# Folding the query weights behind the first and the third quarter of y's matmuls, and the first folded block copied out ahead of the spreading of post_ln

## What is computed

```python
h = tok(x)                         # rms_norm(2560) @ w1.T -> silu(gate) * value (512) @ w2.T -> rms_norm (1024)
h = h + attn(layernorm(h))         # 32 heads, low-rank queries (256) and keys/values (64), rotary halves, causal
h = h + ffn(layernorm(h))          # 1024 x 1024 base + 8 experts of rank 16, weighed by a router

# in attn:
q = rmsnorm(x @ wq_a.T, q_a_ln_w) @ wq_b.T            # per head 64 without and 64 with rotation
ckv, k_pe = split(x @ wkv_a.T)
kv = rmsnorm(ckv, kv_a_ln_w) @ wkv_b.T                # per head k_nope 64, v 128
scores = q_full @ k_full.T * scale ; out = softmax(scores) @ v ; return out @ wo.T
```

## Time and profile before

| | |
|---|---|
| median of 3 executions | 2593.61 us (2593.51 to 2594.55) |
| the profiled execution | 2587.67 us, span 2586.0 us, granted TensorE clock 0.974 |
| TensorE matmul busy | 2431.7 us, 94% of the span, 15004 matmuls |
| VectorE, ScalarE, GpSimd busy | 1635.5, 1187.8, 1000.5 us |
| DMA | 313.61 MB, 121 GB/s over the span |
| `tok_down` | about 640 to 965 us of the span |

### The profile page before, as it was taken

The page is one execution under the profiler, slowest core; times in us unless marked ns, Lnnn a source line. Parts: engine busy times, 40 slices in busy tenths (PEclk is TensorE's granted clock), DMA queues, the critical chain, the costliest instruction groups (busy, mean ns, idle before and its releaser), DMA issues. The chain is left out here.

```text
span 2586.0 us, 45893 instructions
## 1 busy us (share of the span) xinstructions
PE 2431.7 (94%) x15004; PEld 2111.5 (82%) x15004; DVE 1635.5 (63%) x3318; ACT 1187.8 (46%) x3624; POOL 1000.5 (39%) x852
## 2 busy tenths in 40 slices
PE   8999999986899988999999999799999997999998
PEld 6888878865566658999999999688888885899998
DVE  8875587894366657888888898511111113777775
ACT  5664444441345548999999999511111111111110
POOL 5764676772023226667666767100000001011110
PEclk9999999998899999999999999899999998999999
DMA  7654587676466541111111111533333333212211
GB/s 249 201 173 142 184 257 244 209 229 226 136 197 201 194 149 67 46 44 47 40 47 43 47 45 39 198 113 98 97 97 97 97 97 102 69 66 73 75 65 49
DMA packets 202314, 313.61 MB, mean 121 GB/s; under 512 B 20784, under 2 KB 157488, under 8 KB 202032
## 3 DMA queue, kind: packets, MB, share of 16 engines
q1 hardware_dynamic: 194256, 282.54, 34.2%
q0 software_dynamic: 7184, 25.69, 2.5%
q10 hardware_dynamic: 720, 3.67, 0.4%
HBM read 230.05 MB, written 81.79 MB: 121 GB/s over the span
## 5 line engine op out<-in xcount | busy, mean ns | idle before, releaser
L1871 POOL TENSOR_TENSOR ffn_res<-shared_h,ffn_bias 128x1024 f32<-128x1024 f32 x24 | 60.3, 2516 | 852.4 <-DMA ffn_bias<-base_b 555.9
L1512 ACT ACTIVATE attn_prob<-attn_prob,attn_bias 94x94 f32<-94x94 f32 x1024 | 366.9, 361 | 43.4 <-DVE attn_bias L1589 42.0
L740 PE MATMUL up_ps<-up_t_lo,up_s_hi 128*128 128x502 f32 (+1 forms) x840 | 333.5, 397 | 23.2 <-DVE up_t_lo L655 23.1
L741 PE MATMUL up_ps<-up_t_hi,up_s_lo 128*128 128x502 f32 (+1 forms) x840 | 329.8, 393 | 0.0
L742 PE MATMUL up_ps<-up_t_hi,up_s_hi 128*128 128x502 f32 (+1 forms) x840 | 329.0, 392 | 0.0
L1721 DVE TENSOR_TENSOR out_x_lo<-out_raw,out_x_hi 128x512 fp32r<-128x512 f32 x96 | 66.5, 692 | 399.3 <-ACT out_x_hi L1706 399.3
L506 POOL TENSOR_TENSOR up_both<-up_raw 128x502 f32<-128x502 f32 (+1 forms) x150 | 240.3, 1606 | 118.3 <-DVE up_t_lo L655 84.9
L1706 ACT ACTIVATE out_x_hi<-out_raw 128x512 fp32r<-128x512 f32 x96 | 60.6, 632 | 434.7 <-PE out_ps_h L243 284.5
L1628 POOL TENSOR_TENSOR attn_prob<-attn_prob,attn_share 94x752 f32<-94x752 f32 x128 | 184.6, 1442 | 179.5 <-DVE attn_share L1597 179.5
L243 PE MATMUL out_ps_h<-out_w_hi,out_x_lo 128*128 128x512 f32 x768 | 238.1, 391 | 11.2 <-DVE out_w_lo L228 11.2
L243 PE MATMUL out_ps_h<-out_w_lo,out_x_hi 128*128 128x512 f32 x768 | 237.3, 390 | 0.0
(11 more groups left out here) (227 smaller groups left out, 5760.5 us busy)
## 6 DMA issues: line engine op xcount, KB each, us to landing
up_raw<-x_f SPq DMA_DIRECT2D x240, 251.0 KB, 3.4
up_w_raw<-w SPq DMA_DIRECT2D x120, 256.0 KB, 4.1
up_raw<-x_f SPq DMA_DIRECT2D x120, 250.0 KB, 3.7
out_raw<-o_t SPq DMA_DIRECT2D x96, 256.0 KB, 4.3
o_t<-attn_o_t SPq DMA_DIRECT2D x128, 188.0 KB, 1.9
shared_ring<-wo SPq DMA_DIRECT2D x32, 512.0 KB, 6.6
y<-down_y POOLq DMA_DIRECT2D x24, 512.0 KB, 3.4
out_y<-y SPq DMA_DIRECT2D x24, 512.0 KB, 5.7
```

Source lines behind the costliest of these rows:

```text
L740: nc.tensor.matmul(o, sh, tl, start=(kk == 0), stop=False)
L741: nc.tensor.matmul(o, sl, th, start=False, stop=False)
L1512: last = nc.scalar.activation(prob[u % NPR][0:SEQ, h, part], prob[u % NPR][0:SEQ, h, part], ACT.Exp, bias=bias[u % 2][0:SEQ, n:n + 1], sca ...
```

## The change

Three edits, all in `tok_down`. On ScalarE `spread()` of the first body moves behind `wq_out`. On TensorE `fold_q(f, 0)` moves from ahead of y to between n = 0 and n = 1, and `fold_q(f, 1)` from between n = 1 and n = 2 to between n = 2 and n = 3. For the late fold and for steps without y, both still stand behind y's place. No instruction is added or taken away. The name of the change also speaks of paired weighing in attention; the diff holds no line of `attention`.

```diff
@@ ScalarE, body(k, m)
-                if isinstance(k, int) and k == 0 and m == CENTRE_AT:
-                    spread()
                 f = fold(k, m)
                 if f is not None:
                     p, b, turn = f
...
                     last.then_inc(f_out, 1)
+                if isinstance(k, int) and k == 0 and m == CENTRE_AT:
+                    spread()
                 s = stage(k, m, D_Y, U, TILES)
@@ TensorE, body(k, m)
                 late = f is not None and first(f[0], 1)
-                if f is not None and not late:
-                    fold_q(f, 0)
                 s = stage(k, m, D_Y, U, TILES)
...
                     for n in range(4):
-                        if n == 2 and f is not None and not late:
-                            fold_q(f, 1)
+                        if n % 2 == 1 and f is not None and not late:
+                            fold_q(f, n // 2)
                         if first(t, 1):
                             ws.wait(pe, n)
                         last = three_pass(nc, outs, g_hi[u][:, n, :], g_lo[u][:, n, :],
...
                     last.then_inc(y_made, 1)
-                if late:
+                if late or (s is None and f is not None):
                     fold_q(f, 0)
-                if late or (s is None and f is not None):
                     fold_q(f, 1)
```

## The result

The changed kernel takes **2584.09 us** (median of 20 executions, 2578.82 to 2587.95), the kernel before 2591.32 in the same comparisons (20, 2584.97 to 2596.76): ratio 0.9970, 95% interval 0.9963 to 0.9978. That is 7.2 us, 0.28%, where 7.7 was forecast.

What follows compares the result with a forecast made beforehand. TensorE was taken to pace `tok_down`, with only its 3.4 us of gaps per 67 us iteration winnable. 6.95 (B steps) + 1.8 (start) - 1.05 (A steps) = 7.7 us off the median 2593.61: 2585.9 us, range 2581.5 to 2591.5.

Steps and rivals of the forecast that it cites:

- A step: Fold step whose step ahead has no fold (m = 2, 5): loss of 0.15 us each, times 7, -1.05 us.
- B step: Fold step directly following a fold (m = 3, 0): 1.39 us won each, in five of eight, 6.95 us.
- The way back: Two B steps at m = 0 where VectorE's loop returns: its "issue" gap stays, gain taken as nothing, 2.8 us left for range.
- The start: First body, step m = 2: `wq_out` no longer behind `spread`, next fold's work earlier, 1.8 us won (0.8 to 2.6).
- rival 3: Nothing won: the gain is lost to other phases of DMAs and fetches in attention; 2593.6 us, 4%.
- Rival 4: Slower: `wq_out` too late for `fold_v(0)` with one quarter as cover; 2606.9 us at 2.2 us lateness, 4%.
- Rival 2: The wait moves on: VectorE's gap is longer or also at loop entry and exit; 2588.7 to 2591.6 us, 21%.
- Rival 1: More won: VectorE's gap shrinks with TensorE's earlier y, start reaches its upper bound; 10.5 to 11.3 us, 2583.1 us, 11%.
- L1190's wait: Sign: the fold's first matmuls wait for ScalarE's `wv_out`, falling from 11.8 us to about 1.5.
- the first `fold_v(0)`: Sign at the stage's start: it stands at about 663.5 in place of 669.50.
- transposes to `fold_v(0)`: Sign on TensorE: this stretch takes 7.8 us in B, 7.7 in A.
- L1198's wait: Sign: the fold's last matmuls wait 3.1 us growing to about 6, all in two places after VectorE's "issue" gaps.

Runs made afterwards that it cites:

- before_look: The kernel before, unchanged, profiled once more for a second look at its B steps: 2589.22 us, a single execution.
- spread_only: The kernel before with only `spread()` moved behind the first `wq_out`, folds in their old places: 2590.72 us, ratio 0.9993 to the kernel before.
- after_again: The changed kernel once more, nothing altered, in a second comparison: 2580.44 us, ratio 0.9951 to the kernel before.
- folds_only: The changed kernel with `spread()` back ahead of the first `wq_out`, so only the folds moved: 2578.64 us, ratio 0.9939 to the kernel before.
- folds_again: The same kernel as folds_only, run once more on one chip with after_again: 2583.35 us, ratio 0.9967 to the kernel before.
- q1_half: The changed kernel with `fold_q(1)` back between n = 1 and n = 2: 2581.04 us, ratio 0.9956 to the kernel before.
- flat_before: The kernel before with VectorE's steps of `tok_down` written out in place of a loop: 2587.11 us, ratio 0.9978 to the kernel before.
- flat_after: The changed kernel with VectorE's steps of `tok_down` written out in full: 2571.97 us, ratio 0.9909 to the kernel before.
- q1_last: The changed kernel with `fold_q(1)` behind all of y, right ahead of `fold_v(0)`: 2576.13 us, ratio 0.9937 to the kernel before.

## Why the prediction was right

Step times over the profiles of all kernels with the one order of folds or the other, in us:

| | before, before_look, spread_only | after, after_again, folds_only, folds_again, q1_half | by the sum |
|---|---|---|---|
| A step | 12.02 | 12.02 | +0.15 |
| B step, the five of seven not on a way back | 13.66 to 15.33, mean 14.22 | 12.26 to 12.42, mean 12.32 | -1.39 |
| B and next, on a way back | 22.33 to 24.95, mean 23.55 | 24.42 to 26.65, mean 25.36 | 0 |
| VectorE's gap there | 5.01 to 6.36 | 5.58 to 6.77 | the same |

*B steps.* The mechanism and its size were right: 13.67 to 12.27 where nothing else happened, 1.40 against 1.39. What the sum didn't have is that the wait of 1.5 us was in some steps followed by a stretch at 1.2 GHz, 1.5 us more: 5 of the 15 B steps of the first column. None of the 25 of the second had one. So the mean gain of a B step was 14.22 - 12.32 = 1.9 and the five brought 9.5 us in the mean, not 6.95. That mean is loose: against the profiles of before, before_look and spread_only one by one it is 7.0, 8.5 and 13.1 us.

*The way back.* "I take nothing", and a range with 2.8 us of gain. The step that failed is this term, set at 0: it left out what a longer wait does to the clock. The gap is VectorE's own, as assumed, and flat_before and flat_after show it. But a TensorE that comes 1.4 us earlier waits 1.4 us longer, 2.5 to 3.7 us in the ten cases of the second column (0 to 1.8 in the first), and behind such a wait came a stretch at 1.2 GHz in all ten. The longer wait alone would be even, since TensorE is as much earlier there; the stretch behind it is what costs. Cost: 25.36 - 23.55 = 1.8 us twice, **-3.6 us** for a term set at 0. Up to 0.4 of it per gap may be that the gaps in the second column are longer in the mean (6.29 against 5.87), by chance or not; that stays open.

*A steps.* "A loss of 0.1 to 0.2" didn't come. y itself did grow as the sum said: with a second fold inside it one more pair starts slowly and one more is slow ahead of a fold, 6.18 us in place of 6.00 without the folds. But behind the transposes y starts after 0.25 us (783.14), where `fold_q(0)` had started after 0.42; the sum had taken 0.30 to 0.42 for y too. The two cancel. Term -1.05, measured 0.
The Trainium skill's rule (TensorEngine Tiling (Array Packing), "Key Properties") that a change of tiling mode drains the array isn't contradicted: ahead of y as well as inside it the 64-row fold stands between full-height matmuls, so the number of changes is the same, and the prediction was wrong to hold the rule against the change. Nor is the slow first pair a sign of it, as the prediction had read it: behind the transposes, which are full-height themselves, the first pair takes 0.55 us too (783.14 to 783.69).

*The start.* 1.8 was forecast. The start took 76.26, 75.62 and 75.67 us in before, before_look and flat_before, and 75.67, 72.15, 75.29 and 72.96 in after, after_again and their two forms with VectorE's loop written out: 75.85 against 74.02, 1.8 us in the mean, with 3.5 us between the best and the worst of the second four. That is agreement by a mean of few: with q1_half (75.63) it is 1.5, and each half alone has about as much (74.23 in spread_only, 74.48 and 74.16 in folds_only and folds_again). `fold_v(1)` came as worked out; what scatters is when the clock comes back to 2.4 GHz: from 676 to 682 us the granted clock is 0.64 in after and 1.00 in after_again.

*Sum.* 9.5 - 3.6 + 0 + 1.8 = 7.7, less 0.4 in the last steps of the stage, where a stretch at 1.2 GHz fell in some profiles: 7.3, against 7.2 measured in the first comparison and 11.6 in the second, of six executions. That sum and measurement meet so closely is chance. The stage is 319.6 to 326.4 us long in the three profiles of the table's first column and 313.1 to 319.8 in the five of the second, 6.4 us less in the mean; what is left of the span is 2263 to 2268 us in all of them, the same in the mean within 0.3 us, so nothing is won or lost in the other stages (rival 3). The forecast of 7.7 was right in its total since an underrated gain and a missed loss, both by the clock, cancelled: the mechanism of the B steps was right, the total was luck.

The signs that the prediction named: L1190's wait fell to 0.7 us (about 1.5 was named), the first `fold_v(0)` stands at 663.27 (663.5), transposes to `fold_v(0)` is 7.84 in B (7.8) and 7.59 in A (7.7). L1198's wait is 13.0, not about 6: the prediction had left out the 6.6 us at the start, although its own times there, 663.5 and 671.2, held them; the other 6.4 are in the two places that it named.

Rival 4 (`wq_out` too late for `fold_v(0)`) is refuted: the changed kernel's loop has no wait for it. Rival 2 had the right place, the wait that moves on to `fold_v(1)`, but it stayed at the ways back. Rival 1 asked for a gap of VectorE that shrinks with TensorE's earlier y; the gaps are 5.58 to 6.77 us, not shorter. The name's paired weighing isn't in the diff.

The Trainium skill (Runtime: NRT & Kernel Launch, "Instruction fetch mechanics") says that a taken branch out of the window forces a fetch. The trace agrees so far: gaps of 4.1 to 6.8 us ahead of VectorE's first instruction of a body, in all nine profiles with the loop, none in the four with it written out. That it is the fetch, no run shows.

## What to carry to other kernels

A step that is made shorter on one engine meets the gap of another, so follow the engine to its next wait and ask what that one costs when it is longer: here the wait only moved at two places of seven, and it took the clock with it. Look for "issue" gaps at the first line of a loop body on a secondary engine; writing that engine's steps out was worth about as much as the whole reordering (on the kernel before 6.5 us; the reordering 7 to 12; both together 19 to 22, by medians of comparisons that differ by several us among themselves). And when a kernel has short waits that now and then cost clock, one profile is a draw: three profiles with the old order of folds had 0, 1 and 4 of five plain B steps with a stretch at the slow clock.

## What the runs showed of the hardware that I had not expected

- TensorE's clock can fall behind a wait of only 1.5 us: of 15 such waits outside the ways back, 5 were followed by a stretch at 1.2 GHz that cost 1.5 us, the others by none (with flat_before, 6 of 20). Behind waits of 2.5 to 3.7 us it fell in 10 of 10; behind the waits of 0.7 to 0.8 us of q1_last, 14 of them behind the start of the stage, never.
- VectorE's way back through a loop of six written-out steps cost 4.1 to 6.8 us each time, of no fixed length; ScalarE and TensorE showed no such gap at theirs (in before ScalarE's `g_hi` starts 0.15 us after the start of the body's last copy, and TensorE waits 1.60 us for `wv_out` there, 1.52 elsewhere). Where VectorE goes from the written-out body into the loop there was no gap either (in before `g_lo` at 735.11 follows `qn_lo` at 734.78); behind the loop's last round a wait for y would hide one.
- Executions of one kernel scatter by up to 16 us (before: 2584.86 to 2600.69 in one comparison), fifteen times what the first three executions had let me expect (2593.51 to 2594.55). Comparisons of six executions gave 0.9939 and 0.9967 for the same kernel.
